# Routed adapters: seven block products per pair of items instead of a full up projection per item

## The reference

```python
h = jnp.einsum('bsh,bhk->bsk', hidden_states, W_down[role]) + b_down[role][:, None, :]
h = jax.nn.gelu(h, approximate=False)
u = jnp.einsum('bsk,bkh->bsh', h, W_up[role]) + b_up[role][:, None, :]
y = hidden_states + u
mean = jnp.mean(y, axis=-1, keepdims=True)
var = jnp.mean(jnp.square(y - mean), axis=-1, keepdims=True)
yn = (y - mean) * jax.lax.rsqrt(var + LN_EPS)
return yn * gamma[role][:, None, :] + beta[role][:, None, :]
```

## Time and profile before

| what | value |
|---|---|
| runs | median 2880.53 us of 3 (2876.06 to 2884.1) |
| profiled execution | span 2885.1 us (its only time on the page), 58,496 instructions |
| TensorE busy | 2809.6 us, 97%, 12,292 matmuls |
| VectorE / ScalarE / GpSimd busy | 2156.6 (75%) / 908.6 (31%) / 906.2 us (31%) |
| mean granted TensorE clock | 0.993 |
| DMA | 564.20 MB, mean 196 GB/s |

### The profile page before, as it was taken

How to read it: one execution, slowest core, us unless ns; L and a number is a source line. 1 busy time by engine, 2 the same in 40 slices (tenths; PEclk the granted TensorE clock), 3 DMA queues, 4 the chain that set the end, 5 groups by cost and what they waited for, 6 DMA issues and landing times.

```text
span 2885.1 us, 58496 instructions
## 1 busy us (share of the span) xinstructions
PE 2809.6 (97%) x12292; PEld 2317.0 (80%) x12292; DVE 2156.6 (75%) x2611; ACT 908.6 (31%) x1315; POOL 906.2 (31%) x791
## 2 busy tenths in 40 slices
PE   5999999998999999999989999999989999999998
PEld 3888888887888888888768888888878888888886
DVE  4777777777877777777677777777777777777776
ACT  2333333333333333333233333333333333333332
POOL 2333333332333333333233333333333333333332
PEclk8999999999999999999999999999999999999999
DMA  7555655658555565565766556566675565555663
GB/s 191 191 192 189 202 188 194 197 191 247 188 195 193 192 200 188 192 202 188 218 201 203 191 192 196 191 196 194 213 229 194 193 197 190 193 196 193 194 196 133
DMA packets 415620, 564.20 MB, mean 196 GB/s; under 512 B 46496, under 2 KB 308768, under 8 KB 415264
## 3 DMA queue, kind: packets, MB, share of 16 engines
q1 hardware_dynamic: 194080, 292.71, 34.2%
q10 hardware_dynamic: 221184, 268.53, 26.9%
HBM read 359.73 MB, written 201.33 MB: 194 GB/s over the span
## 4 chain that ended last, share of the span: by engine, by line
PE 89%; DMA 4%; DVE 2%; ACTq 2%; issue 1%; ACT 1%; DVEq 0%; SPq 0%; POOLq 0%; POOL 0%
PE pU L399 45%; PE pD L384 44%; DMA hq<-htok 2%; DMA htok<-hg 2%; ACTq L490 1%; DVE y L630 1%; DVE xT L568 1%; DVE wul L559 0%; DMA rwd<-in_Wd 0%; ACTq L190 0%; ACT wdh L417 0%; DVEq L190 0%; ACT xh L431 0%; ACTq L495 0%; ACTq L497 0%
## 5 line engine op out<-in xcount | busy, mean ns | idle before, releaser
L384 PE MATMUL pD<-wdh,xh 128*128 128x512 f32 x2048 | 800.5, 391 | 32.5 <-DVE wdl L545 16.8
L399 PE MATMUL pU<-wuh,hh 128*128 128x512 f32 x2048 | 802.4, 392 | 28.1 <-DVEq L594 18.7
L349 POOL TENSOR_TENSOR xt<-xt,cbu 128x1024 f32<-128x1024 f32 x256 | 616.0, 2406 | 652.9 <-DVE hb L608 620.7
L399 PE MATMUL pU<-wul,hh 128*128 128x512 f32 x2048 | 801.0, 391 | 0.0
L399 PE MATMUL pU<-wuh,hl 128*128 128x512 f32 x2048 | 800.7, 391 | 0.0
L384 PE MATMUL pD<-wdl,xh 128*128 128x512 f32 x2048 | 799.0, 390 | 0.0
L384 PE MATMUL pD<-wdh,xl 128*128 128x512 f32 x2048 | 798.7, 390 | 0.0
L359 POOL TENSOR_TENSOR var<-ssq,heps 128x1 f32<-128x1 f32 x256 | 125.8, 492 | 1252.6 <-ACT sq L470 1252.6
L431 ACT ACTIVATE xh<-xT 128x1024 fp32r<-128x1024 f32 x256 | 262.9, 1027 | 770.2 <-PE pD L384 665.7
L384 PEld LDWEIGHTS pD<-wdh,xh 128*128 128x128 f32 x2048 | 385.5, 188 | 117.1 <-issue 30.9
L399 PEld LDWEIGHTS pU<-wuh,hh 128*128 128x128 f32 x2048 | 387.3, 189 | 114.0 <-issue 18.3
(11 more groups left out here) (49 smaller groups left out, 1179.4 us busy)
## 6 DMA issues: line engine op xcount, KB each, us to landing
out<-ot ACTq DMA_DIRECT2D x256, 512.0 KB, 4.1
xq<-in_x SPq DMA_DIRECT2D x512, 128.0 KB, 3.6
xt<-in_x SPq DMA_DIRECT2D x128, 512.0 KB, 3.5
htok<-hg ACTq DMA_DIRECT2D x256, 256.0 KB, 3.4
hq<-htok ACTq DMA_DIRECT2D x1024, 64.0 KB, 2.8
xq<-out SPq DMA_DIRECT2D x512, 128.0 KB, 3.6
xt<-out SPq DMA_DIRECT2D x128, 512.0 KB, 3.4
rwd<-in_Wd SPq DMA_DIRECT2D x32, 256.0 KB, 7.1
```

The source lines that it names most:

```text
L349: eng.tensor_tensor(xt[:, u.slot(XB), :], xt[:, u.slot(XB), :], cbu[:, :], ALU.add).then_inc(s_r, 1)
L384: last = eng.matmul(pD[:, :], a[:, b, 128 * k:128 * k + 128], w[:, k, :], start=(n == 0), stop=(n == 23))
L399: last = eng.matmul(pU[:, K * m:K * m + K], a[:, v.slot(2), 128 * k:128 * k + 128], w[:, k, K * m:K * m + K], start=(n == 0), stop=(n == 11))
```

## The change

Items of one adapter are now taken in pairs (`Pair`). A layer has `NP` = 65 pairs: a group of odd size is filled up with a repeated item. Both items' h, each cut into two halves of 256, form a 2 x 2 block matrix of 128 x 256 blocks; the up weights form a 2 x 2 matrix of 256 x 512 blocks. Their product is computed by seven block products instead of eight (Strassen's scheme in Winograd's form), each two blocks deep and three matmuls for the precision, 6 matmuls. The left factors need four sums of 256 columns (`sums`, on GpSimd, in `cs`), the right factors four differences of weights, made once for each adapter. Four products use the PSUM bank `bX` in turn, two `bZ`, one `bY`; VectorE adds a bank to the rows `xt` after a product, seven additions of 512 columns a pair.

TensorE's step i now puts a quarter of a down projection of pair i (6 matmuls) between the products of pair i-2. `hT` lies in SBUF instead of PSUM and holds both items. The normalisation is spread: VectorE's `scale` (mean and gamma), ScalarE's `normal` (rstd), GpSimd's `shift` (beta), in place in `xt`, six rows deep. Stores move from ScalarE's queue to SyncE's; bias and gamma loads to GpSimd's and ScalarE's. The result of layer one goes to an own buffer `mid` in pair order. The down weights come through a buffer of two quarters, the loop body has six pairs.

```diff
+NP = NB // 2 + 1
+NSLOT = 2 * NP
+NPH = 2 * NP
+XB = 6
+M = 6
...
+            def shift(p, e):
+                if p.exists():
+                    k = p.slot(e)
+                    count(eng, s_z, p, 2, e + 1)
+                    eng.tensor_tensor(xt[:, k, :], xt[:, k, :], cgb[:, 1, :], ALU.add).then_inc(s_o, 1)
+            def residual(p, e):
+                if p.exists():
+                    k = p.slot(e)
+                    eng.wait_ge(s_x[k], p.lap(3) * 16)
+                    eng.tensor_tensor(xt[:, k, :], xt[:, k, :], cbu[:, :], ALU.add).then_inc(s_r, 1)
+            def sums(p):
+                if p.exists():
+                    a1, a2 = hT[:, 0, 0:256], hT[:, 0, 256:512]
+                    b1, b2 = hT[:, 1, 0:256], hT[:, 1, 256:512]
+                    count(eng, s_hl, p + -1, 4, 3)
+                    count(eng, s_sq, p + -2, 2, 2)
+                    count(eng, s_H, p, 2, 2)
+                    eng.tensor_tensor(cs[:, 0, :], b1, b2, ALU.add).then_inc(s_S, 1)
+                    count(eng, s_S, p, 4, 1)
+                    eng.tensor_tensor(cs[:, 1, :], cs[:, 0, :], a1, ALU.subtract).then_inc(s_S, 1)
+                    eng.tensor_tensor(cs[:, 2, :], a1, b1, ALU.subtract).then_inc(s_S, 1)
+                    count(eng, s_S, p, 4, 2)
+                    eng.tensor_tensor(cs[:, 3, :], a2, cs[:, 1, :], ALU.subtract).then_inc(s_S, 1)
...
+            def step(i):
+                u = i + -2
+                norm(u + -1, 1)
+                shift(u + -1, 0)
+                when_new(eng, i + -1, await_bu)
+                residual(i + -1, 0)
+                shift(u + -1, 1)
+                if not u.first():
+                    when_new(eng, u, load_gb)
+                residual(i + -1, 1)
+                if not i.first():
+                    when_new(eng, i, load_bu)
+                sums(i + -1)
+                when_new(eng, u, take_gb)
+                norm(u, 0)
...
+            def product(u, n, left, bank, start):
+                if u.exists():
+                    count(eng, s_wu, u, 7, n + 1)
+                    for c in range(2):
+                        for m, (a, w) in enumerate(((hh, wuh), (hh, wul), (hl, wuh))):
+                            last = eng.matmul(bank[:, :], a[:, left, 128 * c:128 * c + 128], w[:, n, c, :],
+                                              start=(start and c == 0 and m == 0), stop=(c == 1 and m == 2),
+                                              skip_group_check=True)
+                    last.then_inc(s_P, 1)
+            def step(i):
+                u = i + -2
+                count(eng, s_hl, u, 4, 1)
+                count(eng, s_v, u, 7, 0)
+                product(u, 0, 0, bX, True)
+                down(i, 0, 0)
+                count(eng, s_hl, u, 4, 2)
+                product(u, 1, 2, bZ, True)
+                down(i, 0, 1)
+                count(eng, s_v, u, 7, 1)
+                product(u, 2, 3, bX, False)
+                down(i, 0, 2)
+                product(u, 3, 1, bY, True)
+                down(i, 0, 3)
+                count(eng, s_hl, u, 4, 3)
+                count(eng, s_v, u, 7, 3)
+                product(u, 4, 4, bX, False)
+                down(i, 1, 0)
+                product(u, 5, 5, bZ, False)
+                down(i, 1, 1)
+                count(eng, s_hl, u, 4, 4)
+                count(eng, s_v, u, 7, 5)
+                product(u, 6, 6, bX, False)
+                down(i, 1, 2)
+                down(i, 1, 3)
...
+            def load_h(p, e):
+                if p.exists():
+                    eng.wait_ge(s_hs[e], p.times(16, 16))
+                    count(eng, s_H, p + -1, 2, e + 1)
+                    for a in range(4):
+                        eng.dma_start(hq[32 * a:32 * a + 32, e, :, :],
+                                      htok[e, :, 128 * a:128 * a + 128].rearrange("(b j) n -> j b n", j=32))\
+                           .then_inc(s_hq[e], 16)
...
+            def normal(p, e):
+                if p.exists():
+                    n, k = 2 * (p.c % 2) + e, p.slot(e)
+                    count(eng, s_rs, p, 2, e + 1)
+                    count(eng, s_n, p, 2, e + 1)
+                    eng.activation(xt[:, k, :], xt[:, k, :], ACT.Copy, scale=rstd[:, n:n + 1]).then_inc(s_z, 1)
...
+            def step(i):
+                u, w = i + -2, i + -1
+                when_new(eng, i, take_wd)
+                high_x(i, 1)
+                normal(u + -1, 0)
+                gelu(w, 1)
+                if not i.first():
+                    when_new(eng, i, load_bd)
+                normal(u + -1, 1)
+                load_h(w, 1)
+                when_new(eng, u, take_wu_2)
                 if w.exists():
...
+                    count(eng, s_P, u, 7, 4)
+                    count(eng, s_H, w, 2, 1)
+                    eng.activation(hh[:, 0:2, :], hT[:, 0, :].rearrange("p (a n) -> p a n", a=2), ACT.Copy)\
+                       .then_inc(s_hh, 1)
+                    count(eng, s_S, w, 4, 2)
+                    eng.activation(hh[:, 2:4, :], cs[:, 0:2, :], ACT.Copy).then_inc(s_hh, 1)
+                high_x(i + 1, 0)
+                gelu(i, 0)
+                when_new(eng, w, take_wu_0)
+                if w.exists():
+                    count(eng, s_P, u, 7, 6)
+                    count(eng, s_S, w, 4, 4)
+                    eng.activation(hh[:, 4:6, :], cs[:, 2:4, :], ACT.Copy).then_inc(s_hh, 1)
+                load_h(i, 0)
+                when_new(eng, w, take_wu_1)
+                square(u, 0)
+                if w.exists():
+                    count(eng, s_P, u, 7, 7)
+                    count(eng, s_H, w, 2, 2)
+                    eng.activation(hh[:, 6, :], hT[:, 1, 256:512], ACT.Copy).then_inc(s_hh, 1)
+                square(u, 1)
...
+            def onto(u, n, bank, e, m):
+                if u.exists():
+                    count(eng, s_r, u, 2, e + 1)
+                    count(eng, s_P, u, 7, n)
+                    eng.tensor_tensor(half(u, e, m), bank[:, :], half(u, e, m), ALU.add).then_inc(s_v, 1)
...
+            def step(i):
+                u, w = i + -2, i + -1
+                bias(w, 1)
+                when_new(eng, i, take_wd)
+                scale(u + -1, 1)
+                onto(u, 1, bX, 0, 0)
+                low_x(i, 1)
+                onto(u, 2, bZ, 1, 1)
+                transpose_x(i + 1, 0)
+                onto(u, 3, bX, 0, 1)
+                when_new(eng, u, take_wu_2)
+                transpose_h(w, 1)
+                last_onto(u, 4, bY, 0, 0, 1)
+                low_h(w, 0, slice(0, 2), hT[:, 0, :].rearrange("p (a n) -> p a n", a=2))
+                bias(i, 0)
+                same_wd(i + 1)
+                low_h(w, 1, slice(2, 4), cs[:, 0:2, :])
+                last_onto(u, 5, bX, 1, 1, 2)
+                low_x(i + 1, 0)
+                transpose_x(i + 1, 1)
+                new_or_same_wu(w)
+                last_onto(u, 6, bZ, 0, 1, 3)
+                mean(u, 0, 6)
+                low_h(w, 2, slice(4, 6), cs[:, 2:4, :])
+                when_new(eng, w, take_wu_1)
+                last_onto(u, 7, bX, 1, 0, None)
+                mean(u, 1, 7)
+                low_h(w, 3, slice(6, 7), hT[:, 1, 256:512].rearrange("p (a n) -> p a n", a=1))
+                transpose_h(i, 0)
+                when_new(eng, u, await_gb)
+                scale(u, 0)
```

More of the change, by code:

```diff
@@ new lines, in step, with one @@
+            def step(i, ahead, now, behind):
+                when_new(eng, i, down_rest)
+                for e in range(2):
+                    store(i + -3, e, behind)
+                load_blocks(i + 2, 0, ahead)
+                when_new(eng, i, up_weights)
+                load_rows(i, 0, now)
+                load_rows(i, 1, now)
+                when_new(eng, i + 1, down_first)
+                load_blocks(i + 2, 1, ahead)
+            def one(c):
+                step(Pair(c), int(c + 2 >= NP), int(c >= NP), int(c - 3 >= NP))
@@ L366, in _ @@
+            steps(eng, step, 0, NPH + 3)
         @block.tensor
@@ L373, in body, with down @@
+            def down(i, e, q):
                 if i.exists():
[L374 to L386 removed]
@@ L404, in _ @@
-            steps(eng, body)
+                    if q == 0:
+                        count(eng, s_xl, i, 2, e + 1)
+                        count(eng, s_hb, i + -1, 2, e + 1)
+                    if e == 0:
+                        count(eng, s_wd, i, 4, q + 1)
+                    for k in (2 * q, 2 * q + 1):
+                        for n, (a, w) in enumerate(((xh, wdh), (xh, wdl), (xl, wdh))):
+                            last = eng.matmul(pD[e][:, :], a[:, e, 128 * k:128 * k + 128], w[:, k, :],
+                                              start=(k == 0 and n == 0), stop=(k == 7 and n == 2))
@@ L406, in _ @@
+            steps(eng, step, 0, NPH + 2)
         @block.scalar
@@ L500, in _, with high_wu @@
-            steps(eng, body)
-            for k in range(OB):
-                eng.wait_ge(s_st[k], 16 * NU // OB)
```

(7 more changed lines are left out.)

828 lines of the change are left out of this document (387 added, 441 removed).

## The result

The changed kernel takes **3724.62 us** (median of 4 runs, 3719.24 to 3730.77) against 2878.47 (median of 4) of the kernel before: a ratio of 1.294, 95% interval [1.291, 1.296]. The forecast was 3460 with a range of 3150 to 3680: the sign is right, the time is above the range. The profiled execution spans 3721.4 us.

A forecast was written before the change was run, and what follows sets the result against it. TensorE bounded the kernel before; after the change a loop of waits between in-order queues, Loop A, would decide at 25.4 us a pair. Start 86 + 129x25.4 + adapter changes 84 + end 11 = 3458, rounded to 3460 us, range 3150 to 3680.

The forecast's parts named there:

- Loop A: Chain from VectorE's scaling through GpSimd's additions and sums, h's write and read-back, to the next scaling: 25.4 us a pair.
- stands before products 3, 7 and 1: TensorE waiting for VectorE's additions onto bank bX, together 5.0 us a pair.
- the rival in which TensorE keeps the pace: Both loops under TensorE's 20.4 us a pair, so the kernel gets faster, 2813 us; chance 4%.
- The write of h, 2.7 us: Gelu result's transfer to DRAM within Loop A, taken as the middle of 3.4 (body) and 2.0 (quiet end).
- The collision that I added, 0.9: GpSimd's first shift waiting while VectorE's second scaling, with two SBUF inputs, runs: 0.9 us of Loop A.
- low parts would collide: VectorE's low parts of h meeting GpSimd's sums: another 0.7 us, making Loop A 26.1 us a pair.
- a spread order: If the new order spreads its transfers, the write of h would be near 2.0 us and Loop A 24.7.
- Loop B: VectorE's two transposes of h, each behind its own DRAM round trip, in one step, independent of GpSimd: 21.1 us a pair.
- break-even: The pair length at which the changed kernel would equal the one before: 21.0 us, with 181 us for the rest.
- The rest, 181: Time outside the pair periods: start 86, three later changes of adapter 84, end 11 us.
- The changes of adapter: Each later change: VectorE passes 18.3, exposed ScalarE passes 3.1, 7 for the weight quarters, 28 us in round numbers.
- The clock: TensorE's granted clock, expected 1.00; rival: a quarter of the pairs at 1.2 GHz, 3950 us, chance 5%.

The follow-up runs named there:

- experiment 4: Changed kernel with the low part of h left out of the block products, 76 matmuls a pair instead of 90: 3713.65 us, 1.289 of the kernel before.
- experiment 1: Changed kernel with SyncE's two row loads issued behind the last block loads, at the end of its step: 3428.15 us, 1.190 of the kernel before.
- experiment 5: Changed kernel with the read-back of h taken from an input tensor, without waiting for the write: 3407.81 us, 1.183 of the kernel before.
- experiment 6: Changed kernel with VectorE's low parts of h reading one PSUM operand instead of two SBUF operands: 3700.64 us, 1.285 of the kernel before.
- experiment 3: Changed kernel with SyncE's row loads behind the last block loads and GpSimd's sums behind the first residual: 3511.72 us, 1.220 of the kernel before.
- experiment 7: Changed kernel with GpSimd's four residual and shift additions on one column instead of 1024: 3312.59 us, 1.150 of the kernel before.
- experiment 8: Changed kernel with ScalarE's gelu of item 0 and its write ahead of the high parts of sums and x: 3491.28 us, 1.212 of the kernel before.
- experiment 12: Changed kernel with ScalarE, GpSimd, VectorE reordered and row loads late, plus ScalarE's second normalisation ahead of the read-back issues: 3030.06 us, 1.051 of the kernel before.

## Why the prediction was wrong

- **What bounds.** Right. Loop A holds the kernel, TensorE is out of it (experiment 4), its stands before products 3, 7 and 1 are there (3.83, 0.60 and 0.69 us in the period shown), it is 79% busy as forecast, and the rival in which TensorE keeps the pace is refuted.
- **The write of h, 2.7 us: the step that failed.** It took 5.97 in the period shown, 5.92 on average in the first layer and 3.65 in the second. I had taken the middle between the rows for the body and the quiet end, as if the load on the memory were spread; I never placed the two 512 KB row loads in the walk, and they stood right in front of it. The diff says where SyncE issues them, and its queue was one of those that I should have walked. Over 129 periods these averages are 2.1 us a pair above my 2.7, 270 us, and the sum for the profiled span (3458) fell short by 263. Experiments 1 and 5 each give it back: 296 and 317 us.
- **The other terms of Loop A.** Without the write the period is 27.92 - 5.97 = 21.95, where I had 25.4 - 2.7 = 22.7. The four additions (9.74 for 9.62), sums, high parts and issues fit within 0.6 us each. The collision that I added, 0.9, is no term: the shift starts 1.22 after the normalisation, and is only longer by 0.3. The exclusion itself shows elsewhere, where it costs little (experiment 6).
- **What hangs on the Trainium skill.** By "SBUF — State Buffer", section "Who interferes with whom", low parts would collide with GpSimd and a period be 26.1. The trace agrees on the collision (2.43 us beside an addition, where 0.68 is the row of the same kind of instruction alone) and not on its price. By "DMA: Bandwidth & Descriptors", section "Latency and other measured facts", a spread order would have put the write near 2.0; in the order as it stands it was three times that, and in experiment 1 2.04.
- **Loop B, 21.1.** Mis-sized as well. I closed it over VectorE alone. It closes over ScalarE's order and GpSimd's sums and takes about 24 (experiments 3 and 7; experiment 8 has the same length by another way, its page gives GpSimd 2% of the chain and the transfers 30%). It was not decisive, but would have told that mending Loop A alone can't reach break-even.
- **The rest, 181.** It is 232. The start was right: the first product begins at 85.9 us (86). The changes of adapter are 40 each (28), 36 us more in all; the end, from the last product, is 14 (11); some 12 us I can't place. I had added up the work of a change. The trace shows that a change stretches four pairs to a length of its own: from `bY` to `bY` over four pairs, the three changes take 149.9, 146.2 and 143.4 us in the changed kernel and 145.2, 147.4 and 148.3 in experiment 12. Four ordinary pairs take 112 and 105 in the one and some 82 in the other, so the same stretch costs about 40 us there and 65 here, and shortening the pairs doesn't shorten a change.
- **The clock.** I said that less than 0.95 in the body would prove me wrong, and expected 1.00. It is 0.92 in the first layer and 0.95 in the second, with TensorE at 1.2 GHz for some matmuls after its longest stand; since TensorE waits in the loop anyway, it cost nothing that a run shows (experiment 4: 0.86 and no slower).

The sum of the miss, on the profiled span: 129 periods of 27.05 on average in place of 25.4 are 212 us, the rest 51: 263.

Open: what within a change of adapter takes its 145 to 150 us, what the sequencers wait for at the loop's turn, and how far an order still better than experiment 12's would go.

## What to carry to other kernels

Removing 6% of the matmuls from an engine that is 97% busy pays only if every loop through the other queues is shorter than the new, shorter period; here GpSimd's long additions, two round trips through DRAM and a queue of loads lay in them. Walk every queue, the one that only issues loads too, and give a small transfer in the loop the length that it has behind whatever was issued just before it. And list all the loops: mending the longest one gave back only as much as the distance to the next. Look at single periods too: a mean of 21.2 us hid that five pairs in six already ran close to TensorE's pace.

## What the runs showed of the hardware

- A 256 KB write took 5.97 us when the issue of 1 MB of loads had begun on another engine's queue 1.7 us before it. Over the first layer the loads began a median of 0.5 us before it and it took 5.95; in the second 2.2 us before, and it took 3.36. With the loads moved it took 2.04. Being on another queue did not keep the write apart from them.
- VectorE and GpSimd, both reading SBUF: a 512-wide VectorE pass with two SBUF inputs took 2.43 us beside a GpSimd addition against 0.68, and the 256-wide GpSimd addition behind it 1.19 against 0.74.
- A jump back to the start of the loop body was followed by nothing in VectorE's sequencer for 0.26 us in the kernel before, 2.90 in the changed one and 3.98 in experiment 12 (medians); on GpSimd it was 0.1 to 0.2 us in all three.
- TensorE after its stand of 3.83 us in the changed kernel (the row's spacing goes from 0.23 to 0.43 us, 2.4 and 1.2 GHz):

```profile
1307.05 0.39 PE L422 MATMUL pD<-wdh,xl 128*128 128x512 f32 x1
1311.27 0.79 PE L432 MATMUL bX<-wuh,hh 128*128 128x512 f32 x1 [3.83 <-DVE xt L752]
1311.85 0.63 PE L432 MATMUL bX<-wul,hh 128*128 128x512 f32 x1
1312.28 0.63 PE L432 MATMUL bX<-wuh,hl 128*128 128x512 f32 x1
```
